# Cross attention over 4096 context tokens and sixteen routed experts on one Trainium2 core: values projected turned, another order of sums, weighings and max products, and the experts' down products regrouped by rows

## The reference, cut to what matters

```python
q = (x @ Wq + bq).reshape(1, B * N, H, hd)
kv = (cond @ Wkv + bkv).reshape(1, -1, 2, H, hd)
k, v = (kv[:, :, 0], kv[:, :, 1])
q = _fq_sym(q * scale, axis=-1)      # rounded to 127 steps of max |q| over the head's 16
k = _fq_sym(k, axis=-1)
v = _fq_sym(v, axis=2)               # one scale per head and dimension, over the 4096 tokens
attn = jax.nn.softmax(einsum('bhqd,bhkd->bhqk', q, k), axis=-1)
attn = _fq_unsigned(attn, axis=-1)   # rounded to 255 steps of the row's maximum
out = einsum('bhqk,bhkd->bhqd', attn, v) ... @ Wp + bp
```

```python
mid = silu(x @ w_gate) * (x @ w_up)      # 256 x 176 per expert
y = y + weight[:, e] * (mid @ w_down)    # 256 x 256
```

## Time and profile before

| | |
|---|---|
| median of 3 runs | 1680.68 us (1680.52 to 1681.21) |
| the profiled execution, its own time | 1682.14 us |
| its span, first to last instruction | 1680.3 us |
| mean granted clock of TensorE | 0.955 |
| busy: PE, weight loads, DVE, ACT, POOL | 93%, 65%, 61%, 48%, 33% |

### The profile page before, as it was taken

One profiled execution on the slowest core, in us unless ns is written; L12 is line 12 of the kernel. 1 busy time (PEld: TensorE's weight loads), 2 busy tenths in 40 slices (PEclk: granted clock), 3 DMA queues, 4 the chain that ended last, 5 costly groups with the idle time before them and its releaser, 6 DMA issues. The chain is left out here.

```text
span 1680.3 us, 27653 instructions
## 1 busy us (share of the span) xinstructions
PE 1556.0 (93%) x9976; PEld 1098.0 (65%) x9976; DVE 1027.0 (61%) x2088; ACT 809.3 (48%) x2229; POOL 547.5 (33%) x647
## 2 busy tenths in 40 slices
PE   7989999998799879998889999999999889999969
PEld 5655555555565636777658878888888436666657
DVE  5786666641566565675545665444453479999953
ACT  2223555554212437234444454434444488999931
POOL 2263445453000000251143342242230017777710
PEclk9988999998799979998889999999999999999979
DMA  3000000002333140400100000000000343333120
GB/s 138 1 1 27 1 2 2 2 2 88 144 121 133 32 94 26 144 3 1 51 1 1 1 1 1 1 1 1 1 1 1 108 150 114 114 114 114 39 74 8
DMA packets 53548, 78.03 MB, mean 46 GB/s; under 512 B 14755, under 2 KB 31139, under 8 KB 52518
## 3 DMA queue, kind: packets, MB, share of 16 engines
q1 hardware_dynamic: 53414, 76.27, 13.7%
HBM read 76.00 MB, written 0.26 MB: 45 GB/s over the span
## 5 line engine op out<-in xcount | busy, mean ns | idle before, releaser
L718 DVE TENSOR_REDUCE x_row_max<-banks 128x1 f32<-128x512 f32 x256 | 164.7, 686 | 88.3 <-PE banks L406 88.2
L663 ACT ACTIVATE x_v_full<-banks 128x512 f32<-128x512 f32 x256 | 138.9, 594 | 119.0 <-PE banks L435 117.9
L605 POOL CAST x_v_full<-x_v_full 128x1024 int16<-128x1024 f32 x128 | 133.4, 1042 | 142.3 <-ACT x_v_full L663 141.2
L406 PE MATMUL banks<-x_kT,x_qT 32*128 32x512 f32 x512 | 159.5, 669 | 4.0 <-DVE x_row_max L718 3.5
L213 PE MATMUL banks<-a_w_ring,x_normed_T 128*128 128x512 f32 x320 | 146.6, 598 | 4.8 <-DVE a_r L3313 4.8
L2547 PE MATMUL banks<-x_v,ctx_tokens 128*128 128x128 f32 x1088 | 147.1, 276 | 0.0
L435 PE MATMUL banks<-x_qT_shifted,x_kT 32*128 32x256 f32 x1024 | 145.4, 401 | 0.0
L2547 PEld LDWEIGHTS banks<-x_v,ctx_tokens 128*128 128x128 f32 x1088 | 134.1, 192 | 0.5
L2634 POOL TENSOR_TENSOR ctx_tokens<-ctx_tokens 128x512 f32<-128x512 f32 (+1 forms) x48 | 54.5, 1136 | 229.9 <-DVE ctx_tokens L2774 229.9
L2528 PE MATMUL banks<-x_kT,ctx_tokens 128*128 128x512 f32 x256 | 118.9, 608 | 0.0
L2792 DVE TENSOR_REDUCE x_small<-banks 128x1 f32<-128x2048 f32 x32 | 73.3, 2292 | 51.9 <-PE banks L2528 51.9
(11 more groups left out here) (536 smaller groups left out, 3435.4 us busy)
## 6 DMA issues: line engine op xcount, KB each, us to landing
a_w_ring<-in_L_attn_WB_T SPq DMA_DIRECT2D x16, 512.0 KB, 3.6
a_w_ring<-in_L_attn_WC_T SPq DMA_DIRECT2D x16, 512.0 KB, 5.5
f_gate_up<-in_L_ffn_gate_up SPq DMA_DIRECT2D x9, 736.0 KB, 4.2
ctx_tokens<-in_ctx SPq DMA_DIRECT2D x16, 256.0 KB, 5.9
a_w_ring<-in_L_attn_Wth_T SPq DMA_DIRECT2D x8, 512.0 KB, 3.9
a_bias_ring<-in_L_attn_B_bias_perm SPq DMA_DIRECT2D x16, 256.0 KB, 4.9
a_bias_ring<-in_L_attn_C_bias_perm SPq DMA_DIRECT2D x16, 256.0 KB, 6.1
f_w_down<-in_L_ffn_down SPq DMA_DIRECT2D x9, 384.0 KB, 4.7
```

The lines of the kernel that those rows point to most:

```text
L406: return nc.tensor.matmul(k.bank(bank), qt[lo:lo + SLOT, g, b * T:(b + 1) * T], kt[lo:lo + SLOT, g, HALF * i:HALF * (i + 1)], start=True, ...
L605: nc.gpsimd.tensor_copy(er[q % 4], ew[q % 4]).then_inc(s.rounded, 1)
L663: nc.scalar.activation(ew[q % 4][:, e * HALF:(e + 1) * HALF], k.bank(score_bank(n)), ACT.Exp).then_inc(s.scores_taken, 1)
L718: nc.vector.reduce_max(mx[:, p % 2, e, b, i:i + 1], k.bank(bank), AX.X).then_inc(taken, 1)
```

## The change

In the cross attention:

- The values are projected turned: the weights are the stationary operand and 512 tokens move, so a unit is four passes of 512 columns, without a bias product, and the result has the value's dimension on the partitions. ACT adds the bias when it reads the bank; the bias is a new load of 128 x 2 elements of four bytes, issued behind the context and ahead of Wq. The scale is then one number per partition: DVE reduces along the free dimension. ACT multiplies, adds 128 and rounds to int16 (8 instructions of 1024 elements, j = 6 to 13), PE transposes the integers as fp16 bits (64 transposes, eight each at j = 9 to 16), ACT subtracts 128 while reading (8 instructions of 1024 elements). The spreading of the scale, DVE's four multiplications and POOL's four casts are gone.
- Sums and weighings follow the scores by two steps, not three.
- LEAD is 1, not 3: only two steps have a third max product, and a pair's last max product comes at c = 14. SHIFT is 15; the two max products of step 15 are put behind the shift.
- In a step the order was: max, max, four scores. It is: max, two scores, max, two scores.
- The lanes are joined by four plain transposes of 128 x 128; DVE adds the lanes while reading (a reduction), then takes the reciprocal and multiplies. The value scale is applied by ACT when it copies the transposed result (four instructions in place of two). ACT reads a pair's sums at c = 1.

In the experts: `down` handles a pair: first four products of 128 rows (two experts, two halves), then four of 48 rows, the experts alternating. The wait for the banks is now for all four outputs of the pair before.

The diff, cut to its core:

```diff
-    LEAD = 3
+    LEAD = 1
+    MIDDLE = 128.0
...
+                sp.dma_start(bv[:], A["L0_xattn_bkv"].rearrange("(r c p) -> r p c", r=2, p=P)[1], allow_slow_non_contiguous=True).then_inc(s.bv_loaded, 16)
                 sp.dma_start(wq[:], A["L0_xattn_Wq"].rearrange("(c p) n -> p c n", p=P)).then_inc(s.wq_loaded, 16)
...
-        JOIN, SHIFT = 4, 14
+        JOIN, SHIFT = 4, 15
...
+                def project_values(u):
+                    t, c2 = divmod(u, DC)
...
+                    if u >= 2:
+                        pe.wait_ge(s.v_taken, u - 1)
+                    for c in range(DC):
+                        last = nc.tensor.matmul(k.bank(2 + u % 2), wkv[:, c, D + c2 * P:D + (c2 + 1) * P], k.ctxt[:, c, HALF * t:HALF * (t + 1)],
+                                                start=(c == 0), stop=(c == DC - 1))
+                def turn_values(m):
+                    g, half = divmod(m, 2)
+                    pe.wait_ge(s.vi_ready, DC * (g + 1))
...
+                    for i in range(4):
+                        for c in range(DC):
+                            last = nc.tensor.transpose(k.bank(6 + m % 2).bitcast(F16)[:, (i * DC + c) * P:(i * DC + c + 1) * P], vi16[:, c, g, 4 * half + i], identh[:])
...
-                    for b in range(B):
-                        for r in range(2):
-                            last = nc.tensor.matmul(k.bank(max_bank(n), P, 2 * HD, (r * B + b) * 2 * HD), hd[:, p % 2, r, b * T:(b + 1) * T],
-                                                    sel[:, r].rearrange("p e d -> p (e d)"), start=True, stop=True)
+                    for r in range(2):
+                        for b in range(B):
+                            last = nc.tensor.transpose(k.bank(max_bank(n), P, P, (r * B + b) * P), hd[:, p % 2, r, b * T:(b + 1) * T], k.ident[:])
...
-                for q in range(NCH + 3):
+                for q in range(NCH + 2):
                     p, c = divmod(q, CH)
+                    new = list(new_maxes(q)) if q < NCH else []
...
-                        for m in new[0:2]:
-                            for_max(m, q)
+                        early = [] if c == SHIFT else new
                         for i in range(2):
+                            for m in early[i:i + 1]:
+                                for_max(m, q)
                             for e in range(2):
                                 last = scores(q, e, i)
...
-                        for m in new[2:]:
+                        for m in early[2:]:
                             for_max(m, q)
-                    if q >= 3:
-                        sums(q - 3)
-                        weigh(q - 3)
+                    if q >= 2:
+                        sums(q - 2)
+                        weigh(q - 2)
...
                     if c == SHIFT and p + 1 < PAIRS:
                         shift_queries(p + 1)
+                    if c == SHIFT:
+                        for m in new:
+                            for_max(m, q)
...
+                def take_values(u):
...
+                    if u == 0:
+                        act.wait_ge(s.bv_loaded, 16)
+                    act.wait_ge(s.v_in_psum, u + 1)
+                    nc.scalar.activation(vt[:, c2, HALF * t:HALF * (t + 1)], k.bank(2 + u % 2), ACT.Identity, bias=bv[:, c2:c2 + 1]).then_inc(s.v_taken, 1)
+                def round_values(n):
...
+                    nc.scalar.activation(vi[:, c2, g], vt[:, c2, CB * g:CB * (g + 1)], ACT.Copy, bias=MIDDLE, scale=vcol[:, 1, c2:c2 + 1]).then_inc(s.vi_ready, 1)
+                def take_turned_values(m):
...
+                    nc.scalar.activation(vq[:, 4 * m:4 * m + 4].rearrange("p a n -> p (a n)"), k.bank(6 + m % 2).bitcast(I16), ACT.Copy, bias=-MIDDLE).then_inc(s.v_ready, 1)
...
-                def down(e):
-                    p = e // 2
+                def down(p):
...
-                    if e >= 2:
-                        pe.wait_ge(s.out_taken, B * (e - 1))
+                    if p >= 1:
+                        pe.wait_ge(s.out_taken, 2 * B * p)
...
+                    for e in range(2):
+                        for b in range(B):
+                            nc.tensor.matmul(k.bank(6 + e, P, D, b * D), mid[:, p % 2, e, b * T:(b + 1) * T], wd[:, p % PAIR_RING, e], start=(b == 0), stop=False)
                     for b in range(B):
-                        sl = slice(b * T, (b + 1) * T)
-                        last = matmul_acc(nc, k.bank(6 + e % 2, P, D, b * D),
-                                          [(mid[:, p % 2, e % 2, sl], wd[:, p % PAIR_RING, e % 2]),
-                                           (rest[rows(e), p % 2, sl], wd[rows(e), p % PAIR_RING, 2])])
+                        for e in range(2):
+                            last = nc.tensor.matmul(k.bank(6 + e, P, D, b * D), rest[rows(e), p % 2, b * T:(b + 1) * T], wd[rows(e), p % PAIR_RING, 2], start=False, stop=(b == B - 1))
```

More of the change, by code:

```diff
@@ L246, in l0_xattn @@
         ones_b, zeros_b = sb("ones_b", [3, P], BF16), sb("zeros_b", [3, P], BF16)
-        vf = sb("v_full", [P, NKT, D])
+        vt = sb("vT_full", [P, DC, KEYS])
+        bv = sb("b_v", [P, DC])
+        identh = sb("identh", [P, P], F16)
         vq = sb("v_int", [P, NKT, D], F16)
@@ L365, in project_keys, with project @@
                         pe.wait_ge(s.k_taken, j - 1)
-                    project(j, 0, j % 2).then_inc(s.k_in_psum, 1)
-                def project(j, half, bank):
-                    nc.tensor.matmul(k.bank(bank).rearrange("p (i n) -> p i n", i=2), ones_b[:], bparts[:, half].unsqueeze(1).to_broadcast([3, 2, D]), start=True, stop=False)
+                    project(j, j % 2).then_inc(s.k_in_psum, 1)
+                def project(j, bank):
+                    nc.tensor.matmul(k.bank(bank).rearrange("p (i n) -> p i n", i=2), ones_b[:], bparts[:, 0].unsqueeze(1).to_broadcast([3, 2, D]), start=True, stop=False)
                     for i in range(2):
@@ L372, in project @@
                         for c in range(DC):
-                            last = nc.tensor.matmul(k.bank(bank, P, D, i * D), k.ctxt[:, c, a:a + P], wkv[:, c, half * D:(half + 1) * D],
+                            last = nc.tensor.matmul(k.bank(bank, P, D, i * D), k.ctxt[:, c, a:a + P], wkv[:, c, 0:D],
                                                     start=False, stop=(i == 1 and c == DC - 1))
@@ L505, in _ @@
                         transpose_keys(j - 2)
-                    if j == 7:
-                        pe.wait_ge(s.vmax_ready, 1)
-                        pe.wait_ge(s.qT_taken, 1)
-                        for c in range(DC):
-                            last = nc.tensor.transpose(k.bank(6, P, P, c * P), vmax[:, c * P:(c + 1) * P], k.ident[:])
-                        last.then_inc(s.vmaxT_in_psum, 1)
-                    if j == 9:
-                        pe.wait_ge(s.vdiag_ready, 1)
-                        for r in range(2):
-                            for c in range(DC):
-                                last = nc.tensor.matmul(k.bank(7, P, P, r * D + c * P), k.ones[:], vdiag[:, r, c], start=True, stop=True)
-                        last.then_inc(s.vscale_in_psum, 1)
+                    if 9 <= j < 17:
+                        turn_values(j - 9)
                     if 5 <= j:
@@ L634, in _ @@
                         take_keys(j - 2)
-                    if j == 9:
-                        act.wait_ge(s.vscale_in_psum, 1)
-                        nc.scalar.copy(vscale[:].rearrange("p r n -> p (r n)"), k.bank(7)).then_inc(s.vscale_ready, 1)
+                    if 6 <= j < 14:
+                        round_values(j - 6)
+                    if j >= 10:
+                        take_turned_values(j - 10)
                 def take_shifted(p):
@@ L670, in _ @@
                     act.wait_ge(s.attnT_in_psum, b + 1)
-                    nc.scalar.copy(att[:, :, b * T:(b + 1) * T], k.bank(T_BANK[b], P, D).rearrange("p (c t) -> p c t", t=T)).then_inc(s.attnT_ready, 1)
+                    for c in range(DC):
+                        last = nc.scalar.activation(att[:, c, b * T:(b + 1) * T], k.bank(T_BANK[b], P, T, c * T), ACT.Copy, scale=vcol[:, 0, c:c + 1])
+                    last.then_inc(s.attnT_ready, 1)
             @block.vector
@@ L789, in _ @@
                 leave(PAIRS - 1)
-                dve.wait_ge(s.max_taken, join_entry(PAIRS - 1) + 1)
-                for b in range(B):
-                    nc.vector.tensor_tensor(attn[:, b], attn[:, b], vscale[:, 0], ALU.mult).then_inc(s.attn_ready, 1)
                 for b in range(B):
```

118 lines of the change are left out of this document (48 added, 70 removed).

## The result

The changed kernel takes 1643.58 us, the median of four timed runs (1638.91 to 1644.62), against 1680.60 us before: a ratio of 0.9774, 95% interval 0.9761 to 0.9787. The forecast was 1644. Its profiled execution took 1644.62 us (span 1642.8, mean clock 0.957), 37.5 less in span than the one before.

What follows compares the result with a forecast made beforehand. PE was taken to bound the attention loop and the experts, with the stage before the loop mixed. Terms -12, -4.3, -3, +0.8, -2.8, -0.2 and -15.3 sum to -36.8 us, forecast 1644 us; range 1635 to 1659.

Steps and rivals of the forecast that it cites:

- kept back: Before the loop: 2 us held back for waits not seen, making the stage -12.
- pairs: ends, joins, pair 6: In the attention loop: ends of pairs -3, ACT's uncovered copy at pair 6 +0.8, joins -2.8 us.
- +2.7, between +1 and +5: Before the loop: PE waits for the late value bias to about 17.8 us, +2.7, bounds +1 and +5.
- the order amid the scores: In loop steps, one max product amid the scores: products start together already, the bank wait stays, 0 us.
- the loop's start at full clock: First six loop steps: two have three max products; at full clock 13.6 us where it took 17.9, -4.3.
- nothing is won on the clock: Rival before the loop: late b_v, PE at 1.2 GHz afterwards and in the tail; stage -4, 1652 us, chance 0.17.
- the tail: Before the loop, last key projection to first shift: 19 us where it took 26.2, -7, bounds 0 and -9.
- The wait at the end of a pair: Behind a pair's shift: fourth max product waits for DVE, 1.90 us after the first; sums at 2.97, end 3.64.
- One sign: In the profile after: DVE below 60% from 60 to 120 us.
- Rows side by side: Experts' down: 48-row products of two experts overlap, -2.0 us a period; rival without overlap 1652 us, chance 0.17.
- The slower order: Rival in loop steps: second max product 0.26 to 0.53 us late behind two scores; at 0.4, 1686 us, chance 0.05.
- The order removing the steady wait: Rival in the loop: the new order removes the bank wait, about 85 steps 1.82 to 1.75, 1637 to 1638, chance 0.10.

Runs made afterwards that it cites:

- the nine executions: Nine executions of eight kernels with the same instructions up to the first shift; the transposes behind the fourth unit start between 21.1 and 25.7 us.
- the rests by expert: The changed kernel with the experts' 48-row products ordered first, first, second, second expert in place of alternating: 1643.17 us.

## Why the prediction was right, and where it was not

Its terms against the changed kernel's trace, from mark to mark:

| term | forecast | measured |
|---|---|---|
| values, to the sixth key projection (62.42, now 62.19) | -5 | -0.2 |
| key loop (44.9 to 42.0) | -2 | -2.9 |
| last keys to the shift (107.3 to 133.5; 104.2 to 121.7) | -7 | -8.7 |
| kept back | +2 | 0 |
| loop's start (shift to the end of the sixth step, 17.9 to 15.6) | -4.3 | -2.3 |
| pairs: ends, joins, pair 6 | -5.0 | -5.2 |
| last step to the norm (12.3 to 12.6) | -0.2 | +0.3 |
| experts (96.1 to 80.5) | -15.3 | -15.6 |
| all else, not touched | 0 | -3.0 |

**What failed.** The step "+2.7, between +1 and +5", the price of the value bias: it was 7.5 in this trace, by the kernel with the bias first (25.51 less 18.05). The units themselves gave 7.7 of the 8 (the sixth key projection comes at 54.74 with the bias first, before it was 62.42). Of the 7.5, the gap makes 4.4 (the third unit starts at 19.05 in place of 14.62): the load landed at 18.2 us, not 16.9. The row of Wq was no bad guess for it, since in three of the nine executions it landed at 16.7 to 17.0, but it had no spread. The other 3 are the half clock behind the gap, which was put in the bound instead of the sum. In the earliest executions the price is about 3, nearly the forecast. The second is **the order amid the scores: 0**. In the steady steps it nearly is, but at the loop's start the old order ran 1.4 and 3.1 us longer, with a longer half clock. The third is **the loop's start at full clock**: I laid out steps of 1.9 and 2.3, and the stretch ran at 0.71. It gave 2.3 and not 4.3. (The terms listed for it add up to 13.3, not 13.6, and of the +5 for turning the values the sums use only 3 and 1: two slips of 0.3 and 1 us.) The rival "nothing is won on the clock" came true in its first half, the late load with half clock behind it, but not in its second: the tail ran at 0.97, and the three stretches before the loop gave 11.8 together, where the rival had 4 and my sum 12. That this stage came out is luck: 4.8 us too little in its first term, against 0.9, 1.7 and the 2 kept back in the others.

**What made up for it.** The 2 us kept back weren't needed, the tail gave 1.7 more, and 3.0 came from code that the change does not touch (0.9 in the mixer, 2.3 in the last 80 us of the program, and in between 2.5 lost behind the experts and 2.3 won again). What it touches gave 34.5, which against the median would be 1646.2.

**What held.** Transposes of the values take 0.54 for eight, 0.067 each (0.08 taken). The wait at the end of a pair came out to 0.02 us. Joins are 0.59 for 1.01. DVE lost 19.9 us up to the first shift (20 said) and ACT got 16.6 (17); ACT, of which I was afraid, has 54% of the key loop. One sign failed all the same: DVE was to be below 60% from 60 to 120 us and has 72% there (43.5 us). The experts came out to 0.3 us, with their bank wait of 1.84 at the end.

**The rivals.** Rows side by side: shown, in both orders. The slower order falls. The Trainium skill, "TensorE: Matmul & The Clock Gate", Part 3, says matmuls are strictly first in, first out; the scores at 255.05, ahead of a second pass at 255.58, and the rests by expert speak against it once more. The order removing the steady wait falls too: 1.88 and 1.74 still take turns.

Still open: why the old order keeps the clock down longer at the loop's start, and how much of the 1.4 and 3.1 us it costs by itself. The later scores and the lower clock came together in the traces, and no run parts them.

## What to carry to other kernels

When a small load becomes something that an engine waits for, its place in the queue is part of the change: put it ahead of the bulk. Count how many products use a ring of banks in a row with nothing between; moving other work of the same engine between them takes the wait away for nothing. And read single stretches of two traces before believing a sum of medians: here 4 to 5 us of a median were clock in code that nobody had touched.

## What the runs showed of the hardware that I had not expected

The same instructions behind a gap of about 3 us of PE ran at half clock in one execution and at full clock in another (6.62 and 3.67 us for eight passes). A load of 256 elements of four bytes each landed 2.6 us after its issue when it stood first, and 13.2 us behind 4 MB of context. Products of 48 rows at partitions 0 and 64 ran side by side even with two products of the same rows ahead of them (1.07 us for 8 passes).
